# Mix 2 moved forward, projection and second layer in other PSUM banks, and the second norm's squares on GpSimd

## The reference, cut to what matters

```python
x = x + conv_block(ln_c(x))      # ln_c: over the 48 channels of a pixel, eps 1e-6
t = to_tokens(x)                 # a token is a pixel
t = t + ffn(ln_t(t))             # ln_t: over the 48 channels of a token, eps 1e-5
```

## Time and profile before

| | |
|---|---|
| median of three runs (lowest to highest) | 692.02 us (691.2 to 693.7) |
| the profiled execution, its own time | 691.75 us |
| span from first to last instruction in it | 689.9 us |
| mean granted TensorE clock over the span | 0.985 of full speed |
| busy: PE / DVE / ACT / POOL | 663.6 / 595.6 / 534.6 / 458.3 us |

### The profile page before, as it was taken

How to read it: one execution, slowest core, us unless ns; L and a number is a source line. 1 busy time by engine, 2 the same in 40 slices (tenths; PEclk the granted TensorE clock), 3 DMA queues, 4 the chain that set the end, 5 groups by cost and what they waited for, 6 DMA issues and landing times.

```text
span 689.9 us, 19144 instructions
## 1 busy us (share of the span) xinstructions
PE 663.6 (96%) x6604; PEld 525.4 (76%) x6604; DVE 595.6 (86%) x1159; ACT 534.6 (77%) x1086; POOL 458.3 (66%) x348
## 2 busy tenths in 40 slices
PE   6789999999999999999999999999999999999984
PEld 5567787887778878777878787778778877787751
DVE  6668898899988988999889889998988899877887
ACT  3234588988888889888888888888888888777784
POOL 4535667687777777876777778767777787753353
PEclk9999999999999999999999999999999999999995
DMA  4544444554445545544454455445544554342102
GB/s 102 99 112 123 122 103 115 146 141 125 119 118 135 136 114 136 140 128 108 122 141 127 114 143 139 124 107 124 145 118 125 141 141 111 99 123 74 44 24 69
DMA packets 52207, 80.73 MB, mean 117 GB/s; under 512 B 20823, under 2 KB 36079, under 8 KB 52111
## 3 DMA queue, kind: packets, MB, share of 16 engines
q1 hardware_dynamic: 49823, 78.30, 44.2%
q10 hardware_dynamic: 2288, 1.20, 0.7%
HBM read 63.17 MB, written 16.30 MB: 115 GB/s over the span
## 4 chain that ended last, share of the span: by engine, by line
PE 88%; DVE 3%; issue 2%; POOL 2%; DMA 1%; ACT 1%; SPq 1%; DVEq 0%; POOLq 0%; ACTq 0%
PE inva L542 18%; PE invb L549 16%; PE mixp L529 13%; PE misc L558 8%; PE misc L819 8%; PE misc L629 4%; PE misc L529 4%; PE misc L673 3%; PE misc L778 3%; PE misc L578 3%; PE misc L587 2%; PE misc L663 2%; PE mixp L642 2%; PE mixp L649 2%; POOL st L1596 1%
## 5 line engine op out<-in xcount | busy, mean ns | idle before, releaser
L1596 POOL TENSOR_TENSOR st<-st,neg_half 128x16 f32<-128x16 f32 x32 | 92.8, 2901 | 118.6 <-DVE st L1502 118.5
L542 PEld LDWEIGHTS inva<-inv,gmix 128*127 128x127 f32 x1024 | 123.3, 190 | 24.9 <-DVE gmix L1274 12.8
L542 PE MATMUL inva<-inv,gmix 128*127 128x128 f32 x1024 | 141.0, 280 | 0.2 <-DVE gmix L1274 0.2
L1274 DVE TENSOR_TENSOR gmix<-mixp,freq_w 128x508 f32<-128x508 f32 x192 | 122.5, 679 | 15.9 <-PE mixp L529 15.9
L549 PE MATMUL invb<-inv,gmix 128*127 128x128 f32 x1024 | 134.7, 274 | 0.1
L549 PEld LDWEIGHTS invb<-inv,gmix 128*127 128x127 f32 x1024 | 126.1, 191 | 2.1 <-DVE hbuf L1285 0.5
L912 ACT ACTIVATE hid<-misc 128x512 f16<-128x512 f32 x180 | 93.9, 595 | 17.6 <-PE misc L629 17.6
L1630 POOL TENSOR_TENSOR st<-st,neg_half 128x16 f32<-128x16 f32 x31 | 95.5, 3080 | 16.3 <-DVE st L1353 16.3
L1285 DVE TENSOR_TENSOR hbuf<-gact,invb 127x512 f32<-127x512 f32 x128 | 87.3, 682 | 21.3 <-ACT gact L904 16.7
L904 ACT ACTIVATE gact<-inva 127x512 f32<-127x512 f32 x128 | 77.1, 603 | 21.8 <-PE inva L542 21.2
L921 ACT ACTIVATE hid<-hid 128x512 fp8e5<-128x512 f16 x174 | 93.2, 618 | 0.0
(11 more groups left out here) (187 smaller groups left out, 1332.6 us busy)
## 6 DMA issues: line engine op xcount, KB each, us to landing
taps<-cz_scratch SPq DMA_DIRECT2D x63, 292.2 KB
xres<-in_x_dram SPq DMA_DIRECT2D x64, 192.0 KB, 4.3
xin<-in_x_dram SPq DMA_DIRECT2D x63, 192.0 KB, 3.4
out_dram<-ob SPq DMA_DIRECT2D x60, 192.0 KB, 2.6
taps<-cz_scratch SPq DMA_DIRECT2D x63, 146.1 KB
crm<-rm_scratch SPq DMA_DIRECT2D x58, 96.0 KB
cx<-in_x_dram SPq DMA_DIRECT2D x32, 96.0 KB
cz_scratch<-cz SPq DMA_DIRECT2D x63, 48.8 KB
```

Of the source, the lines that this page charges most:

```text
L542: mm = pe.matmul(inva[0:HID, q * PX:(q + 1) * PX], gmix[:, s % 2, q, 0:HID], inv[:], start=True, stop=True, skip_group_check=True)
L1274: dve.tensor_tensor(gmix[:, s % 2, 2 * q:2 * q + 2, 0:HID2], pair[q][:, 0:2 * HID2].rearrange("p (e c) -> p e c", e=2), freq_w[:], ALU.mul ...
L1596: pool.tensor_tensor(st1[:, 6, :], st1[:, 5, :], neg_half[:], ALU.pow).then_inc(pow1, 1)
```

## The change

- Mix 2 stands directly behind mixes 0 and 1 and writes `bank[2..3]`; `gmix` has four slots, no longer two.
- The projection writes `mixp`, the second layer `bank[0..1]`, each after DVE has weighed what stood there.
- The first layer's groups go into other banks and another order on PE: c=0 group 2 between the halves of inverse 1 as before, c=0 groups 0 and 1 behind `stream`, c=1 groups 0 and 1 behind mix 3, then `convolve`, then c=1 group 2. ACT's copies of them (`accumulator`) and DVE's relus follow; the last group's copy and relu move into the next step.
- `stream` writes `bank[1]` (band 3 on).
- ACT no longer squares. POOL makes `tsq` as one product of `tpix` with itself, ahead of `output`; `second_norm` is as it was.
- On DVE the sum of the first norm's squares and `weigh(t, 0)` stand ahead of `gate(t, 4, 3)`, `weigh(t, 2)` and `gate(t, 3, 0)` ahead of `bias`.
- SP issues `rows_in` ahead of the output store. ACT's `order_x` stands ahead of `sums`.

```diff
-        gmix = sb("gmix", [128, 2, 4, 256])
+        gmix = sb("gmix", [128, 4, 4, 256])
...
+        mix_pair = (mixp, bank[0:2], bank[2:4], mixp)
...
+        MADE = {(0, 2): 1, (0, 0): 2, (0, 1): 3, (1, 0): 4, (1, 1): 5, (1, 2): 6}
+        RELUED = {(0, 2): 1, (0, 0): 3, (0, 1): 3, (1, 0): 5, (1, 1): 5, (1, 2): 6}
+        hid_bank = {(0, 2): bank[0], (0, 0): bank[3], (0, 1): bank[2],
+                    (1, 0): bank[0], (1, 1): bank[3], (1, 2): bank[2]}
... SP, step
+                if live(t, 0) and a > 2:
+                    rows_in(t)
                 if live(t, 6):
                     sp.wait_ge(out_ready, upto(l + 1))
...
-                if live(t, 0) and a > 2:
-                    rows_in(t)
... PE, second_layer
-                pair = mixp
-                pe.wait_ge(gmix_ready, upto(8 * n + 2, 8 * STEPS))
+                pair = bank
...
                 for c in range(2):
+                    pe.wait_ge(gmix_ready, upto(8 * n + 3 + c, 8 * STEPS))
... PE, step
                     mix(t, 1)
+                    pe.wait_ge(hid16_ready, upto(6 * l + 6))
+                    mix(t, 2)
                 if live(t, 4):
-                    project(t, 0, bank[3])
-                    pe.wait_ge(hid16_ready, upto(6 * l + 6))
-                    project(t, 1, bank[2])
+                    pe.wait_ge(gmix_ready, upto(8 * n + 1))
+                    project(t, 0, mixp[0])
+                    pe.wait_ge(gmix_ready, upto(8 * n + 2))
+                    project(t, 1, mixp[1])
...
-                    mix(t, 2)
-                if live(t, 5):
-                    pe.wait_ge(q16_ready, upto(2 * k + 2))
...
-                    hidden(t, 0, 0, bank[0])
-                    hidden(t, 0, 1, bank[1])
...
+                if live(t, 5):
+                    pe.wait_ge(tpix_ready, upto(2 * m + 2, 2 * STEPS))
...
+                    hidden(t, 0, 0, hid_bank[0, 0])
+                    hidden(t, 0, 1, hid_bank[0, 1])
                 if live(t, 3):
...
                     mix(t, 3)
                 if live(t, 5):
+                    pe.wait_ge(hid16_ready, upto(6 * k + 1))
+                    hidden(t, 1, 0, hid_bank[1, 0])
                     pe.wait_ge(hid16_ready, upto(6 * k + 2))
-                    hidden(t, 1, 0, bank[0])
-                    hidden(t, 1, 1, bank[1])
-                    pe.wait_ge(hid16_ready, upto(6 * k + 3))
-                    hidden(t, 1, 2, bank[2])
+                    hidden(t, 1, 1, hid_bank[1, 1])
                 if live(t, 2):
                     convolve(t)
+                if live(t, 5):
+                    pe.wait_ge(hid16_ready, upto(6 * k + 3))
+                    hidden(t, 1, 2, hid_bank[1, 2])
... ACT, rest
-                    act.wait_ge(stat2, upto(4 * m))
-                    act.sem_inc(act_held, 1)
-                    act.activation(tsq[:, 8 * q:8 * q + 8, :], channels(bank[2 + q]), ACT.Square)\
-                       .then_inc(tsq_ready, 1)
... ACT, step, from gelu(t, 3, 0) on
-                    accumulators(t, 0, (0,))
...
-                    accumulators(t, 0, (1, 2))
+                    accumulator(k, 0, 2)
                 if live(t, 3):
                     gelu(t, 3, 1)
... the stream's copy
-                    accumulators(t, 1, range(3))
+                    accumulator(k, 0, 0)
+                    accumulator(k, 0, 1)
+                    accumulator(k, 1, 0)
... DVE, step
+                if live(t, 6):
+                    relu(l, 1, 2, 1)
...
+                if live(t, 0):
+                    dve.wait_ge(xsq_ready, upto(2 * a + 2))
+                    dve.tensor_reduce(st1[:, 1, :], (xsq if a != 1 else tsq)[:], AX_X, ALU.add).then_inc(stat1, 1)
+                if live(t, 3) and not first_mix:
+                    weigh(t, 0)
                 if live(t, 4):
                     gate(t, 4, 3)
...
+                if live(t, 3):
+                    weigh(t, 2)
+                    gate(t, 3, 0)
                 if live(t, 6):
                     bias(t)
-                if live(t, 3):
-                    gate(t, 3, 0)
-                if live(t, 3):
-                    weigh(t, 2)
                 if live(t, 4):
                     second_norm(t)
                 if live(t, 5):
-                    relu(t, 0)
+                    relu(k, 0, 2, 1)
                 if live(t, 3):
                     gate(t, 3, 1)
+                if live(t, 5):
+                    relu(k, 0, 0, 2)
                 if live(t, 3):
                     weigh(t, 3)
                 if live(t, 5):
-                    relu(t, 1)
+                    relu(k, 1, 0, 2)
... POOL, step, behind zpix
+                if live(t, 4):
+                    pool.wait_ge(tpix_ready, upto(2 * m + 2))
+                    pool.wait_ge(stat2, upto(4 * m))
+                    pool.sem_inc(pool_held, 1)
+                    pool.tensor_tensor(tsq[:], halves(tpix)[:, :, 0:CH], halves(tpix)[:, :, 0:CH], ALU.mult)\
+                        .then_inc(tsq_ready, 2)
                 if live(t, 6):
                     output(t)
```

More of the change, by code:

```diff
@@ L522, in mix @@
                     pe.wait_ge(lo_ready, upto(2 * n + 2))
-                pe.wait_ge(gmix_ready, upto(8 * n + 2 * (s if s != 1 else 0)))
-                pair = bank if s == 1 else mixp
+                if s == 0:
+                    pe.wait_ge(gmix_ready, upto(8 * n))
+                pair = mix_pair[s]
                 for e in range(2):
@@ L541, in inverse @@
                 for q in range(4):
-                    mm = pe.matmul(inva[0:HID, q * PX:(q + 1) * PX], gmix[:, s % 2, q, 0:HID], inv[:],
+                    mm = pe.matmul(inva[0:HID, q * PX:(q + 1) * PX], gmix[:, s, q, 0:HID], inv[:],
                                    start=True, stop=True, skip_group_check=True)
@@ L548, in inverse @@
                 for q in range(4):
-                    mm = pe.matmul(invb[0:HID, q * PX:(q + 1) * PX], gmix[:, s % 2, q, HID:HID2], inv[:],
+                    mm = pe.matmul(invb[0:HID, q * PX:(q + 1) * PX], gmix[:, s, q, HID:HID2], inv[:],
                                    start=True, stop=True, skip_group_check=True)
@@ L577, in stream @@
                         src = rows[:, :, 2 * TW * g:2 * TW * (g + 1)].rearrange("p r (i w) -> p i r w", w=TW)
-                        mm = pe.matmul(bank[3][32 * g:32 * g + 32, :], wpc[:, turn, :], src,
+                        mm = pe.matmul(stream_bank(c)[32 * g:32 * g + 32, :], wpc[:, turn, :], src,
                                        start=(turn == 0), stop=(turn == 1), skip_group_check=True)
@@ L866, in last_group @@
                     if live(t, 5):
-                        pe.wait_ge(tsq_ready, upto(2 * m + 1, 2 * STEPS))
-                        hidden(t, 0, 2, bank[2])
+                        if peeled and a == 5:
+                            pe.wait_ge(set_done, 2)
+                        pe.wait_ge(q16_ready, upto(2 * k + 2))
+                        hidden(t, 0, 2, hid_bank[0, 2])
                 if live(t, 3):
@@ L904, in gelu, with accumulator @@
                 act.activation(gact[:, s % 2], inva[0:HID, :], ACT.Gelu).then_inc(gelu_ready, 1)
-            def accumulators(t, c, groups):
-                k = at(t, 5)
-                for g in groups:
-                    act.wait_ge(hid_done, upto(6 * k + 3 * c + g + 1))
-                    act.wait_ge(hid8_ready, upto(6 * (k - 1) + 3 * c + g + 1))
-                    act.activation(hid16[:, 3 * c + g, :], bank[g][:], ACT.Copy).then_inc(hid16_ready, 1)
+            def accumulator(k, c, g):
+                act.wait_ge(hid_done, 6 * k + MADE[c, g])
+                act.wait_ge(hid8_ready, upto(6 * (k - 1) + 3 * c + g + 1))
+                act.activation(hid16[:, 3 * c + g, :], hid_bank[c, g][:], ACT.Copy).then_inc(hid16_ready, 1)
             def activations(k, c, groups):
                 for g in groups:
-                    act.wait_ge(relu_ready, upto(6 * k + 3 * c + g + 1))
+                    act.wait_ge(relu_ready, upto(6 * k + RELUED[c, g]))
                     if c == 0 and g == 0:
@@ L1120, in step @@
                     activations(l, 1, range(3))
+                if live(t, -1) and a != 0:
+                    order_x(t, -1)
                 if live(t, 6):
                     sums(t, range(2))
-                if live(t, -1) and a != 0:
-                    order_x(t, -1)
                 if a == 1:
@@ L1145, in step @@
                     act.wait_ge(stream_done, upto(c + 1))
[L1146 removed]
+                    act.activation(convs[:].rearrange("p u x -> p (u x)"), stream_bank(c)[:], ACT.Copy)\
                        .then_inc(convs_ready, 1)
                 if live(t, 5):
[L1149 removed]
+                    accumulator(k, 0, 0)
+                    accumulator(k, 0, 1)
+                    accumulator(k, 1, 0)
                 if live(t, 2):
@@ L1269, in weigh @@
                 n = at(t, 3)
-                pair = bank if s == 1 else mixp
-                dve.wait_ge(inv_done, upto(8 * n + 2 * s - 2))
```

(12 more changed lines are left out.)

81 lines of the change are left out of this document (46 added, 35 removed).

## The result

The kernel after the change takes 788.31 us (median of 4 runs, 785.83 to 793.15), the kernel before 691.62 (4 runs): a ratio of 1.140, with a 95% interval of 1.134 to 1.146 (the intervals in brackets below are of the same kind). The forecast was 748, its range ended at 767. It named the wait that makes the kernel slower, but the measured time lies 40 us above it and 21 above the range. The profiled execution took 785.83 us, 784.0 of it span, at a mean granted clock of 0.946 (0.985 before).

The account below looks back on a forecast made before the run. PE, busy for 96% of the span, was taken to set the step. 29 steps x (1.91 us of wait at inverse 2 + 0.02 of PE's order) = 56 on 691.75 gave 748 us; 8-in-10 range 703 to 767.

Parts of the forecast that it names:

- Does the step grow by all of it? Yes: PE's wait before inverse 2's second half lengthens each step in full, nothing absorbing it: 21.7 us a step.
- 1.91 + 0.02: Growth per step in us: PE's wait for `gate` before inverse 2's second half, plus PE's own reordered work; 29 steps.
- The point left open: Whether POOL's `output` holds DVE up like its other products: 748 us if so, 692 if not; no change had 0.09.
- -0.21, +0.07 and +0.15: PE's order, us a step: cheaper switches between matmul kinds, then wait (a), then Wait (b); about +0.02 together.
- -0.10 and +0.19: On PE, us a step: c=1 group 2 saves a switch from half-array matmuls, `convolve` now pays one.
- wait (a): On PE, the second layer's c=1 waits for DVE's `weigh(t, 1)`: 0.07 us a step, between 0 and 0.26.
- Wait (b): On PE, c=1 group 1 waits for ACT's copy of c=0 group 0, behind the stream's copy: 0.15 us, 0 to 0.60.
- The third collision: Rival: DVE's L1341, held by the squares, then waits for `output`; PE waits 2.27, 758 us; upper variant within 0.71.
- The taps: Rival: the taps `stream` needs come late, so it waits 0.5 us or more on top, over 762 us; chance 0.04.

Follow-up runs that it names:

- experiment 1: The changed kernel with eight idle matmuls, read by nobody, on PE between the halves of inverse 2: 759.34 us, ratio 1.098.
- experiment 2: The changed kernel with POOL's `output` product cut to an eighth of its columns from the second band on: 713.62 us, ratio 1.032.
- Experiment 3: The changed kernel with both POOL's `output` product and its squares cut to an eighth from the second band on: 696.79 us, ratio 1.0075.
- experiment 4: The changed kernel with the squares back on ACT in place of POOL's product, all else as changed: 704.01 us, ratio 1.018.
- experiment 6: The kernel before with only the squares moved to POOL ahead of `output`, order on PE and banks as before: 740.24 us, ratio 1.071.
- experiment 8: The changed kernel with `gate(t, 3, 1)` on DVE moved into the second norm, ahead of its wait for the squares: 722.61 us, ratio 1.042.
- experiment 7: As experiment 6, with a DVE fill of a scratch tile, some 0.5 us, ahead of `gate(t, 3, 1)`: 790.96 us, ratio 1.140.
- experiment 9: As experiment 8, with the small product of the means (L1373) also moved ahead of that gate on DVE: 720.05 us, ratio 1.038.

## Why the prediction was wrong, point by point

**The step that failed** is "Does the step grow by all of it? Yes", which made 21.7 us a step and 56 us in all. It took PE's work after the wait at the duration it has before, so the sum has no term for the clock. The prediction read the clock as full but for the last slice, but a 9 there means 90% or more, and the first steps of the kernel before already show PE slow behind a wait. Its chain there:

```profile
19.44 1.98 PE misc L605 x8
...
31.19 3.65 PE misc L605 x8
```

Ahead of the second of these groups PE waits 2.10 us for DVE (L1233); its eight matmuls then take 3.65 where the eight of the first take 1.98, and the mean clock is 0.91 from 20 to 40 us, 0.66 from 30 to 35. In mid-kernel PE waits nowhere before, so the durations there hold for a PE that does not wait. With waits of 2 us the clock falls in most steps: 32 us by the mean clock of the profiles, 29.0 by experiment 1. The range left it out too, and so ended below the result.

**The wait, mis-sized.** "1.91 + 0.02" measured 2.1: 1.99 of wait, and 0.10 because the eight matmuls behind a wait take 0.99 instead of 0.89; 29 x 0.17 = 5 us. The remaining microseconds are those of the first steps, for which the sum had no term. 748 + 32 + 5 + 1.7 = 787.

**The mechanism held in each link.** The product took 1.47 (forecast 1.48). L1373 and L1376 ended with `output` and `tcen`, at over 1 us each, and PE's wait was at the second half of inverse 2 behind `gate`. The point left open, whether `output` blocks as the other products do, is settled by experiment 2: it does, and with it cut short one collision and 0.50 of wait are left. The rule cited from the Trainium skill, SBUF — State Buffer, "SBUF: two separate sides", that the two exclude each other for the whole instruction, agrees with operations of 1.22 and 1.40 that end 0.03 to 0.04 behind the POOL products. These rows have DVE held by POOL, not POOL by DVE.

**PE's order** was forecast at +0.02 a step from -0.21, +0.07 and +0.15. Experiment 3 measures 19.78 for the step, as before: the sum is right, but partly by luck. Its chain has mix 2 at 0.87 (1.75 for mixes 1 and 2) and `inva` of inverse 1 at 0.90, as forecast. But the first layer's c=1 and `convolve` take 0.38 + 0.59 + 0.22 = 1.19. In the chain of the kernel before they took 0.54 and 0.44: that is +0.21, where -0.10 and +0.19 were forecast. The second layer takes 0.51 + 0.43 where it took 0.43 + 0.43, 0.08 more, near the 0.07 of wait (a). Wait (b), put at 0.15, is not there with POOL's squares, and the two errors nearly cancel; it is 0.46 with ACT's (experiment 4), inside the bounds of 0 to 0.60.

**The rivals.** The third collision did not happen: the mean (L1367) ran at 316.65, ahead of the squares, in 0.18, and so in 30 of its 31 instances. Where the squares start first, as in experiment 6, they do hold the mean, but it slips in at their end, as the prediction argued: L1338 took 0.78 and ended at 321.43, the squares at 321.40. The taps were not late in the kernel after, where PE waited from 200 to 600 for nothing but the gate; they became late when the gate's wait was gone (experiment 8).

## What to carry to other kernels

Before work is moved to an engine that is 66% busy, look at what its long instructions hold up: here 1.5 us on POOL cost 2 us on PE, because three back-to-back POOL products made two 0.17 us operations of DVE wait in front of the one that PE needs. A forecast that ends in a recurring wait of PE needs a second sum, with PE's work behind the wait at the lower clock; the wait's own length is then only a part of the price, and filling it with matmuls that nobody reads got 29 of 97 us back. Cut the suspected instruction to an eighth, as in experiments 2 and 3: that prices one link of such a chain and leaves the order alone.

## What the runs showed of the hardware that was not expected

- The granted clock fell to 0.50 for 3.4 us behind waits of PE of 1.99 us (after) and 2.03 us (experiment 7), in most steps but not in all (19 and 22 such stretches for 29 steps with a wait), and never behind those of 1.45 us (experiment 6). Such a step is up to 1.66 us longer. Why some waits of one length are followed by it and others not, no run here tells.
- Not only operations on two tensors are held: L1381, a TENSOR_SCALAR on one 128x16 tensor, took 1.40 beside `tcen` (experiment 9) and 0.17 elsewhere. The sum of squares, a TENSOR_REDUCE, took 0.95 beside `output`, and the like sum L1493 of the kernel before 0.94 with POOL idle.
- POOL's product of a tile with itself took 1.47, as long as that of two tiles of the same size (1.48).
